# A fourth split value group, paired additions on GpSimd, and output weights split early, in a cross-attention kernel

## The reference, cut to what matters

```
k, v  = keys and values of [context 4096 tokens ; own 256 tokens]   # 4 key-value heads of 128
q     = rope(rms_norm(x @ wq))                                      # 16 heads of 128
w     = softmax(q @ k.T / sqrt(128) + causal mask on the own tokens)
attn  = (w @ v) for each of the 16 heads, side by side              # 256 x 2048
x     = x + attn @ wo                                               # wo: 2048 x 512
```

## Time and profile before

| What | us |
| --- | --- |
| time, median of 3 runs (lowest to highest) | 988.67 (988.24 to 989.04) |
| the profiled execution: its time, its span | 988.25, 986.5 |
| PE matmul busy | 971.4 (98%) |
| PE weight loads busy | 856.5 |
| DVE busy | 776.1 |
| ACT busy | 612.3 |
| POOL busy | 560.7 |

### The profile page before, as it was taken

One profiled execution on the slowest core, in us unless ns is written; L12 is line 12 of the kernel. 1 busy time (PEld: TensorE's weight loads), 2 busy tenths in 40 slices (PEclk: granted clock), 3 DMA queues, 4 the chain that ended last, 5 costly groups with the idle time before them and its releaser, 6 DMA issues.

```text
span 986.5 us, 15792 instructions
## 1 busy us (share of the span) xinstructions
PE 971.4 (98%) x5695; PEld 856.5 (87%) x5695; DVE 776.1 (79%) x1179; ACT 612.3 (62%) x1026; POOL 560.7 (57%) x517
## 2 busy tenths in 40 slices
PE   9999999999999999999999999997999999999998
PEld 8888888889899999999999999976788988888887
DVE  6654667545988888888888988999698877777775
ACT  5443344336767777677776677682498566666663
POOL 4643444331499999999999999996001132222222
PEclk9999999999999999999999999999999999999999
DMA  7557654566304130222105041310700785555540
GB/s 293 182 167 249 214 184 135 171 214 226 117 1 133 50 107 2 86 97 58 50 13 170 28 146 49 118 54 1 278 21 1 282 292 204 187 181 184 188 160 22
DMA packets 56525, 131.10 MB, mean 133 GB/s; under 512 B 4192, under 2 KB 36352, under 8 KB 55424
## 3 DMA queue, kind: packets, MB, share of 16 engines
q1 hardware_dynamic: 56448, 130.09, 38.9%
HBM read 101.21 MB, written 28.87 MB: 132 GB/s over the span
## 4 chain that ended last, share of the span: by engine, by line
PE 91%; DVE 4%; POOL 2%; issue 1%; ACT 1%; DMA 1%; SPq 0%; DVEq 0%; POOLq 0%
PE bank L526 18%; PE bank L600 17%; PE bank L629 17%; PE bank L508 13%; PE bank L928 9%; PE bank L930 5%; PE bank L736 1%; PE bank L535 1%; PE bank L623 1%; POOL first_max L1926 1%; PE bank L625 1%; PE bank L627 1%; DVE weights L1122 1%; DVE first_max L1088 1%; PE bank L792 1%
## 5 line engine op out<-in xcount | busy, mean ns | idle before, releaser
L600 PE MATMUL bank<-qT_hi,kT 128*128 128x256 f32 (+1 forms) x1088 | 295.2, 345 | 0.6 <-ACT weights L1631 0.6
L1926 POOL TENSOR_TENSOR first_max<-first_max,weights 128x512 f32<-128x512 f32 x214 | 278.9, 1303 | 20.7 <-PE bank L629 0.4
L629 PE MATMUL bank<-weights,vN 128*128 128x256 f32 (+1 forms) x896 | 258.4, 375 | 0.0
L1631 ACT COPY weights<-bank 128x512 f32<-128x512 f32 (+1 forms) x272 | 154.8, 580 | 99.9 <-PE bank L600 58.0
L600 PEld LDWEIGHTS bank<-qT_hi,kT 128*128 128x128 f32 x1088 | 196.1, 189 | 19.4 <-ACT weights L1631 1.2
L1096 DVE TENSOR_TENSOR first_max<-bank,first_max 128x512 f32<-128x512 f32 x196 | 134.9, 688 | 35.1 <-ACT weights L1631 29.8
L1122 DVE TENSOR_TENSOR weights<-weights,bank 128x1024 f32<-128x1024 f32 x128 | 155.0, 1211 | 1.8 <-PE bank L656 1.8
L600 PE MATMUL bank<-qT_lo,kT 128*128 128x256 f32 (+1 forms) x544 | 153.6, 282 | 0.0
L1635 ACT ACTIVATE weights<-weights 128x1024 f32<-128x1024 f32 x144 | 144.5, 1003 | 10.5 <-DVE weights L1122 9.5
L526 PE MATMUL bank<-w_ctx_hi,ctx_hl 128*128 128x512 f32 x512 | 144.7, 394 | 0.3 <-ACT w_ctx_hi L1594 0.3
L629 PEld LDWEIGHTS bank<-weights,vN 128*128 128x128 f32 x896 | 141.5, 189 | 3.0
(11 more groups left out here) (262 smaller groups left out, 1730.1 us busy)
## 6 DMA issues: line engine op xcount, KB each, us to landing
e_raw<-in_experts SPq DMA_DIRECT2D x51, 768.0 KB, 4.4
k_spill<-k_stage SPq DMA_DIRECT2D x16, 1024.0 KB, 5.5
kT<-k_spill SPq DMA_DIRECT2D x15, 1024.0 KB, 5.2
v_spill<-v_stage SPq DMA_DIRECT2D x16, 512.0 KB, 6.8
vN<-v_spill SPq DMA_DIRECT2D x16, 512.0 KB, 3.5
ctx_raw<-in_ctx SPq DMA_DIRECT2D x15, 512.0 KB, 4.2
w_raw<-in_w_qkv SPq DMA_DIRECT2D x6, 1024.0 KB, 5.1
comb<-c_spill SPq DMA_DIRECT2D x8, 512.0 KB, 6.0
```

Of the source, the lines that this page charges most:

```text
L600: done = e.matmul(dst, kT[:, w, kt * P:(kt + 1) * P], qT[a][:, h, q0:L], start=m == 0, stop=m == 2)
L629: done = e.matmul(dst[:, q0:L], vN[:, kt, :], weights[:, cols], start=kt == 0, stop=kt == KTILES - 1)
L1631: e.copy(s_buf[h % 2][:, g, 0:width(g)], bank[SCORE_BANKS[s % len(SCORE_BANKS)]][:, 0:width(g)]).then_inc(taken, 1)
L1926: e.tensor_tensor(run_sum[:, :], run_sum[:, :], here, ALU.add).then_inc(summed, 1)
```

## The change

Four of the 17 groups are split instead of three, at other places. On POOL the running sum of a head is 1024 wide and takes a quad (two groups) at a time; at the end of a head it is folded twice. In the last head DVE's own sum begins at group 4 instead of 6. The low values have one buffer instead of two. The output weights are split in the context stage: per tile SP loads a chunk of 256 columns, ACT casts it, POOL subtracts, and SP writes both parts to DRAM (`wo_parts`), through three buffers; at the end of the heads `wo_lo` is loaded from there where `wo` was loaded before, and `wo_hi` in four DMAs of 1 MB once the last even head's weights are used up. ACT's 16 casts and DVE's 16 subtractions at the end are gone. Some order constants move. In the diff, `main_of_wo` is ACT's (called at the end of each tile), `rest_of_wo` POOL's (behind `split_ctx`, ahead of a tile's `k_rs`), `move_wo` SP's (ahead of each tile's `spill`); the last lines are SP's, behind its loop over the steps.

```diff
-TURN_AT, REDUCE_AT, SPREAD_AT = (5, 5, 4, 2), (2, 5, 5, 3), (7, 7, 6, 3)
+TURN_AT, REDUCE_AT, SPREAD_AT = (5, 5, 4, 3), (1, 5, 5, 4), (6, 7, 6, 5)
-SOONER = 2
+SOONER = 4
-SUMS = NG + 1
-OWN_SUMS = 6
-SPLITS = (2, 7, 12)
+SUMS = NG // 2 + 3
+OWN_SUMS = 4
+OWN_STEPS = NG + 1 - OWN_SUMS
+SPLITS = (1, 5, 9, 12)
-WO_CASTS, WO_MAIN, WO_LOWS, WO_REST = 241, 243, 246, 249
+WO_MAIN, WO_REST = 246, 250
+WC = DM // 2
+NWC = NH * DM // WC
...
+        wo_chunk = [back.take(f"wo_chunk{i}", [WC]) for i in range(3)]
+        wo_main = [back.take(f"wo_main{i}", [WC], F32R) for i in range(3)]
+        v_low = back.take("v_low", [NKV, BT, HD], F32R)
...
             def project_main(tt, i):
                 h = WO_ORDER[i]
-                pe.wait_ge(wo_hi_done, i + 1)
+                pe.wait_ge(wo_hi_in[h // 4], 16 * NKV + 16)
...
             def project_rest(tt, i):
                 h = WO_ORDER[i]
-                pe.wait_ge(wo_lo_done, i + 1)
+                load = [any(lo <= h < hi for lo, hi in part) for part in WO_LOADS].index(True)
+                pe.wait_ge(*(wo_in[load], 48) if load < KD else (w_xb_in, chunks_in + 32))
...
                 if i // BT in SPLITS:
                     k = SPLITS.index(i // BT)
                     dve.wait_ge(v_copied, i + 1)
-                    if k >= 2:
+                    if k >= 1:
                         dve.wait_ge(self_out, 64 + 16 * k)
-                    e.tensor_tensor(v_low[k % 2][:, :, s, :], bank[2 + z][:, :].rearrange("p (g d) -> p g d", g=NKV), v_stage[slot][:, :, s, :],
+                    e.tensor_tensor(v_low[:, :, s, :], bank[2 + z][:, :].rearrange("p (g d) -> p g d", g=NKV), v_stage[slot][:, :, s, :],
                                     ALU.subtract).then_inc(v_low_done, 1)
...
+            def main_of_wo(c):
+                act.wait_ge(wo_chunk_in[c % 2], 16 * (c // 2 + 1))
+                e.copy(wo_main[c % 3][:, :], wo_chunk[c % 3][:, :]).then_inc(wo_hi_done, 1)
...
+            def rest_of_wo(c):
+                pool.wait_ge(wo_hi_done, c + 1)
+                e.tensor_tensor(wo_chunk[c % 3][:, :].bitcast(F32R), wo_chunk[c % 3][:, :], wo_main[c % 3][:, :], ALU.subtract).then_inc(wo_lo_done, 1)
...
             def fold_sums(h, before):
                 pool.wait_ge(summed, before)
+                e.tensor_tensor(run_sum[:, 0, :], run_sum[:, 0, :], run_sum[:, 1, :], ALU.add).then_inc(summed, 1)
+                pool.wait_ge(summed, before + 1)
...
+                j = g // 2
+                if g == SELF:
+                    here = weights_of(n)
+                    pool.wait_ge(expd, NQUAD * (h + 1))
                     for k, (to, lo, w) in enumerate(((0, 0, L), (P, L, P))):
+                        pool.wait_ge(summed, SUMS * h + j - 1 + k)
+                        e.tensor_tensor(run_sum[:, 0, to:to + w], run_sum[:, 0, to:to + w], here[:, lo:lo + w], ALU.add).then_inc(summed, 1)
+                    fold_sums(h, SUMS * (h + 1) - 2)
+                elif g % 2 and j:
+                    pool.wait_ge(expd, NQUAD * h + j + 1)
+                    pool.wait_ge(summed, SUMS * h + j - 1)
+                    e.tensor_tensor(run_sum[:, :, :], quad(h, 0) if j == 1 else run_sum[:, :, :], quad(h, j), ALU.add).then_inc(summed, 1)
...
+            def move_wo(i):
+                if i >= 3:
+                    sp.wait_ge(wo_parts_out, 32 * (i - 2))
+                if i >= 2:
+                    c = i - 2
+                    h, cols = wo_columns(c)
+                    sp.wait_ge(wo_hi_done, c + 1)
+                    e.dma_start(wo_parts[0][:, h, cols], wo_main[c % 3][:, :].bitcast(F32)).then_inc(wo_parts_out, 16)
+                    sp.wait_ge(wo_lo_done, c + 1)
+                    e.dma_start(wo_parts[1][:, h, cols], wo_chunk[c % 3][:, :]).then_inc(wo_parts_out, 16)
+                if i < NWC:
+                    h, cols = wo_columns(i)
+                    e.dma_start(wo_chunk[i % 3][:, :], t["wo"][:, h, cols]).then_inc(wo_chunk_in[i % 2], 16)
...
+            for j in range(NH // 4):
+                sp.wait_ge(pv, NG * (H15 - 1) + 4 * j + 4)
+                sp.wait_ge(summed, summed_at(H15 - 1, 4 * j + 3))
+                e.dma_start(wo_hi[:, 4 * j:4 * j + 4, :].bitcast(F32), wo_parts[0][:, 4 * j:4 * j + 4]).then_inc(wo_hi_in[j], 16)
```

More of the change, by code:

```diff
@@ L246, in build_program @@
         v_stage = [back.take(f"v_stage{i}", [NKV, BT, HD]) for i in range(2)]
-        v_low = [back.take(f"v_low{i}", [NKV, BT, HD], F32R) for i in range(2)]
+        wo_chunk = [back.take(f"wo_chunk{i}", [WC]) for i in range(3)]
+        wo_main = [back.take(f"wo_main{i}", [WC], F32R) for i in range(3)]
+        v_low = back.take("v_low", [NKV, BT, HD], F32R)
         qreg = region["q"]
@@ L261, in build_program @@
         sp_ = region["spare"]
-        first_max = sp_.take("first_max", [2, GW])
-        run_max, run_sum = first_max[:, 0], first_max[:, 1]
+        running = sp_.take("running", [3, GW])
+        first_max, run_max, run_sum = running[:, 0:2], running[:, 0], running[:, 1:3]
         pt_ = region["pt"].again()
         own_sum = Region(nc, region["k"].base + 4 * NH * DM, 4 * GW).take("own_sum", [GW])
-        own_both = pt_.take("own_both", [L])
+        own_both = sp_.take("own_both", [L])
         pT = [pt_.take(f"pT{i}", [2, GW], F32R) for i in range(RING)]
@@ L365, in build_program @@
         self_out = sem("out_self")
-        k_in, v_in = [sem(f"in_k{i}_then_comb") for i in range(NPIECE)], [sem(f"in_v{i}_then_comb") for i in range(NPIECE)]
-        small_in, w_xb_in = sem("in_small"), sem("in_w_xb_then_wo")
-        w_xa_in, w_z_in, w_out_in = sem("in_w_xa"), sem("in_w_z"), [sem("in_w_out"), x_in]
+        wo_hi_in = k_in = [sem(f"in_k{i}_then_wo_hi_then_comb") for i in range(NPIECE)]
+        v_in = [sem(f"in_v{i}_then_comb") for i in range(NPIECE)]
+        small_in, w_xb_in = sem("in_small"), sem("in_wo_odd_chunks_then_wo_then_w_xb")
+        w_xa_in = sem("in_wo_even_chunks_then_w_xa")
+        wo_chunk_in, chunks_in = [w_xa_in, w_xb_in], 16 * NWC // 2
+        wo_parts_out = w_z_in = sem("out_wo_parts_then_in_w_z")
+        w_out_in = [sem("in_w_out"), x_in]
         e_in, c_out = ctx_in + first_in, sem("out_c")
-        comb_in, comb_total = (k_in + v_in)[:NE // 4], [16 * NKV] * NPIECE + [NKV * n for n in V_LOADS]
+        comb_in, comb_total = (k_in + v_in)[:NE // 4], [16 * NKV + (16 if i < NH // 4 else 0) for i in range(NPIECE)] + [NKV * n for n in V_LOADS]
         ctx_total = [16 * (NBATCH // NCR)] * NCR + [16] * BT
@@ L1156, in finish_head @@
                 e.tensor_tensor(head_out[z][:, :], bank[VALUE_BANKS[z]][:, 0:L], rden_all[:, :], ALU.mult).then_inc(ho, 1)
-            def rest_of_wo(i):
-                h = WO_ORDER[i]
-                dve.wait_ge(wo_hi_done, i + 1)
-                e.tensor_tensor(wo_lo[:, h, :], wo_sb[:, h, :], wo_hi[:, h, :], ALU.subtract).then_inc(wo_lo_done, 1)
             for i in range(NT):
@@ L1614, in act_program @@
                     own_rotate(n)
+                if i:
+                    main_of_wo(i - 1)
             def last_keys():
@@ L1646, in finish_head @@
                 e.copy(outT[0][:, h, :], head_out[h % 2][:, :]).then_inc(oT_hi, 1)
-            def main_of_wo(i):
-                h = WO_ORDER[i]
-                load = [any(lo <= h < hi for lo, hi in part) for part in WO_LOADS].index(True)
-                act.wait_ge(*(wo_in[load], 48) if load < KD else (w_xb_in, 32))
-                act.wait_ge(pv, NG * (H15 - 1) + h + 1)
-                act.wait_ge(summed, summed_at(H15 - 1, h))
-                e.copy(wo_hi[:, h, :], wo_sb[:, h, :]).then_inc(wo_hi_done, 1)
             for s in range(NH * NG + LEAD):
@@ L2018, in spill @@
                     e.dma_start(v_low_spill[:, k].rearrange("g p t d -> p g (t d)"),
-                                v_low[k % 2][:, :, :, :].bitcast(F32).rearrange("p g t d -> p g (t d)")).then_inc(self_out, 16)
+                                v_low[:, :, :, :].bitcast(F32).rearrange("p g t d -> p g (t d)")).then_inc(self_out, 16)
             def spill_self():
@@ L2086, in sp_program @@
             spill(NBATCH - 1)
+            move_wo(NWC)
             for p in (0, 1, 2, NPIECE - 1, NPIECE - 2):
@@ L2089, in sp_program @@
                 load_v(0, p)
+            move_wo(NWC + 1)
             def load_later():
@@ L2108, in sp_program @@
                     for lo, hi in WO_LOADS[g // 4]:
-                        e.dma_start(wo_sb[:, lo:hi, :], t["wo"][:, lo:hi]).then_inc(wo_in[g // 4] if g < SELF else w_xb_in, 16)
+                        e.dma_start(wo_lo[:, lo:hi, :].bitcast(F32), wo_parts[1][:, lo:hi]).then_inc(wo_in[g // 4] if g < SELF else w_xb_in, 16)
                 group, last = h // REP + 1, h % REP == REP - 1 and h < H15
```

49 lines of the change are left out of this document (21 added, 28 removed).

## The result

After the change the kernel takes 1046.28 us (median of 4 runs, 1045.90 to 1046.89), before it 988.86 us (988.24 to 989.72) in the same job: ratio 1.0583, interval 1.0571 to 1.0596. The forecast was 1018.7, range 998 to 1032: the direction was right, and the loss is 57.4 us where 30 were forecast.

What follows compares the result with a forecast made beforehand. PE was taken to bound the kernel nearly everywhere, POOL just behind in the heads. 988.25 + 26.9 (heads) + 8.6 (context) - 5.5 (end) + 0 = 1018.3, as a median 1018.7 us; range 998 to 1032.

Steps and rivals of the forecast that it cites:

- 1, a split group saves PE: Heads: a fourth split group saves PE 0.16 us a head, making its own period 26.81 us.
- 2, 1024-wide addition: Heads, POOL's total work: a 1024-wide addition takes 2.37 us; POOL's total of some 26.2 us a head stays under PE's.
- part 3: Heads, POOL's order: 12.7 us of work before group 1's low part idles PE 2.1 us a head; +26.9 us in all.
- Part 4: Context stage, single low-value buffer: DVE waits at tile 10 for own spills, PE idles 6 and 2 us; +8.6 us.
- Part 5: Context stage, output weights' casts, subtractions and DMAs: hidden, 0 us, bounds 0 and +4.
- Part 6: Last head and end: 10.2 us without work go, new waits cost 4.7; 5.5 us won, bounds 0 and 10.
- start of the heads: Start of the heads, 234 to 262 us: little changes, 0, between -1 and +1.
- rival C: Slower still: additions cost 2.61 us (+10), or the clock falls behind each head's wait; 1029 us, chance 0.14.
- Rival A: Heads, not slower: POOL keeps up between group 12's low part and the next head's group 1; 986.9 us, chance 0.12.
- B: Faster: Rival A, and the own spills have landed when DVE asks in the context stage; 978.3 us, chance 0.04.

Runs made afterwards that it cites:

- low_first: Changed kernel, with POOL making the next head's first low part ahead of the masked group's additions and PE taking the sum one group later: 996.66 us, ratio 1.0072.
- ctx_low_start: The kernel with both repairs, plus the first heads' turn, reduction, spread and subtraction places as in the kernel before: 982.12 us, ratio 0.9934.
- the kernel with both repairs: Changed kernel with low_first's reordering, and DVE at tile 10 waiting only for the first low-value spill: 985.68 us, ratio 0.9970.
- half_filled: Changed kernel, with PE doing four unused products ahead of its wait at group 1 in heads 1 to 14: 1026.80 us, ratio 1.0383.
- low_before_both: Changed kernel, with POOL making the next head's first low part ahead of the last addition only: 1017.52 us, ratio 1.0284.
- extra_add: Changed kernel, with POOL's last fold of each head done twice, lengthening its list by 0.75 us: 1061.28 us, ratio 1.0716.

## Why the forecast missed, step by step

| step | forecast | measured |
|---|---|---|
| 1, a split group saves PE | 0.16 us a head | 0.19 (26.97 to 26.78, low_first) |
| 2, 1024-wide addition | 2.37 us | 2.386 |
| 3, list of POOL | 12.7 us | 12.74 |
| 3, wait of PE at group 1 | 2.1 us | 2.03 |
| 3, price in the heads | +26.9 us | +48.4 (13 steady heads) |
| 4 and 5, context stage | +8.6 and 0 | +10 and +2.1 |
| 6, end | -5.5 us | -6.6 |
| start of the heads | 0 (-1 to +1) | +4.1 |

**The step that failed is the price of part 3.** "A head takes 28.9 instead of 26.97 us": the wait, its place, its length and its cause are there in the trace, and with the wait filled the head takes 29.09. But PE works at its lower clock for 3.41 us behind each wait and loses 1.60 us more. Over the 13 steady intervals that is 20.8 of the 27.6 us by which the forecast was short. The lower clock behind the wait was put at nothing there. The mechanism stood in rival C with the right place ("the clock falls to its lower level behind the waits at each head"), at a chance of 0.14 shared with another cause, and its price of some 10 us in all was not worked out from a row. It could have been: the only fall of the kernel before, around the idle piece of 4.51 us, lasted 3.4 us, and half of that, 1.7 us, times 14 is 24 us. What the trace of before could not tell was whether 2.1 us of waiting would do it: its wait of 1.75 us at 652.4 has no fall behind it. In doubt, the case deserved far more than 0.14, and the range should have reached 1043. The Trainium skill (TensorE: Matmul & The Clock Gate, section HAM oscillation — how this bites in real kernels) describes a kernel whose matrix engine waits for a DMA once a tile and starts each tile at the lower clock. The trace agrees in kind, with heads in the place of tiles: 3.4 us at half clock in every steady head. But the waits of the kernel described there are some 3 to 5 us long; here waits of 2.03 us did it.

**Part 3, the rest.** 29.09 instead of 28.9 is 0.2 us a head, 2.5 us in all. The other way, the wait comes in 13 steady heads and not in 14, 1.9 us less.

**Part 4** was right in place and cause, and 1.1 us short at the turn (9.7 instead of 8.6). Most of that is the start: SP issues the last write-out at 92.14 instead of 91.57, behind the DMAs of the output weights, and DVE starts at 98.31, not at 97.4. The second idle piece that it foresaw on PE is missing. In its place PE works at half clock from 99.66 to 104.9, which costs about as much (2.6 us, an estimate: half of these 5.2).

**Part 5** had a cost, 2.1 us, inside its bounds of 0 to +4. A wait of 0.65 us on PE for ACT's copy of the context near the stage's end is part of it; I did not take it apart further. The subtractions took 1.06 us on the average and not 0.77.

**Part 6** was near in number (6.6 won, 5.5 forecast), by misses of opposite sign. The wait for the first quarter of wo_hi was right, 2.35 us (forecast 2). The wait of 2.7 us for the low part in head 15 did not come. But the 1.8 us of lower clock, counted as won, were not: the fall at 715.9 again lasts 3.4 us, and the granted clock of the stretch is 0.97 as before. PE's idle time in it fell from 8.4 to 3.3 us; the remaining 1.4 us of the gain are not accounted for.

**The start** was named with nearly no cost and lost 4.1 us; ctx_low_start shows that 2 to 4 us of it lie in the places of the first heads.

**Rival A**, POOL by totals keeping up, was wrong for this order of the list and right for that of low_first; B, the same without the stall, was to take 978.3, and the kernel with both repairs took 985.7: between them lie the start of the heads (some 4), part 5 (2.1), and an end that won 1.6 less than rival A had put (6.6 against 8.2).

## What to carry to other kernels

A queue with time to spare over a whole round can still be the bound in one stretch of it. Here an instruction that PE waits for stood behind work that could have come later, in a list of 12.7 us. Its place cost 50 us, and the same additions in another order cost none of it: look at the longest run of work between two results that another engine needs. Price a wait of TensorE that comes back every round twice, as the idle time and as the slower clock that may follow it, and take both from rows. And where one count serves several writers, as self_out does, a buffer less can make an engine wait for transfers that have nothing to do with the buffer.

## What the runs showed of the hardware

- Waits of 1.2 us (half_filled) and 1.36 us (low_before_both) in each head brought no fall of the granted clock. Waits of 2.03 us brought one in each head (3.41 us at half), and waits of 2.83 us in extra_add one in each head, every third of 6.8 us. At the heads' end the clock also falls behind shorter waits: in ctx_low_start at 653.4, with waits of 1.34 and 0.82 us within 2 us of each other. So the length of one wait alone doesn't tell.
- Nine products that nobody uses made the kernel 17.7 us faster than the changed one, since they cover a wait. low_first, which takes the wait away, is 49.6 us faster; the filler is a measuring device and no repair.
- POOL's addition of two fp32 operands took 0.77, 1.30 and 2.39 us at 256, 512 and 1024 columns. The Trainium skill (GPSIMD Engine Reference, section 3.1, Elementwise — side-by-side cycle accounting) gives 4497 ns for 2048 columns. Half of it, 2.25 us, is an estimate for the last; the measured value is 6% above it.
